# Query projection of a cross attention by row tile in place of by batch, and the last value projection moved ahead of the third sums

## The reference

```python
def _L0_xattn_ref(x, context, Wq, Wk, Wv):       # NHEADS = 32, HEAD_DIM = 16
    q = x @ Wq.T
    k_raw, v_raw = context @ Wk.T, context @ Wv.T
    q = q.reshape(b, n, NHEADS, HEAD_DIM).transpose(0, 2, 1, 3)
    kv = jnp.concatenate([k_raw, v_raw], axis=-1).reshape(b, m, NHEADS, HEAD_DIM, 2)
    k, v = (kv[..., i].transpose(0, 2, 1, 3) for i in range(2))
    q = _rmsnorm(q)                                # over the 16 of a head
    k = _rmsnorm(k)
    attn = jax.nn.softmax(jnp.einsum('bhnd,bhmd->bhnm', q, k) * scale, axis=-1)
    out = jnp.einsum('bhnm,bhmd->bhnd', attn, v)
```

## Time and profile before

| | us |
|---|---|
| Median of 3 runs | 1402.93 (1398.98 to 1403.82) |
| The profiled execution: its time | 1401.41 |
| its span, first to last instruction | 1399.3 |
| PE busy in the span | 1315.0 (94%), 10968 matmuls |
| DVE busy | 780.1 (56%) |
| ACT busy | 641.5 (46%) |
| POOL busy | 274.1 (20%) |
| Mean granted clock of PE | 0.984 |

### The profile page before, as it was taken

How to read it: one execution, slowest core, us unless ns; L and a number is a source line. 1 busy time by engine, 2 the same in 40 slices (tenths; PEclk the granted TensorE clock), 3 DMA queues, 4 the chain that set the end, 5 groups by cost and what they waited for, 6 DMA issues and landing times.

```text
span 1399.3 us, 27527 instructions
## 1 busy us (share of the span) xinstructions
PE 1315.0 (94%) x10968; PEld 868.8 (62%) x10968; DVE 780.1 (56%) x1938; ACT 641.5 (46%) x1452; POOL 274.1 (20%) x266
## 2 busy tenths in 40 slices
PE   4779999999999999999999999999999789999996
PEld 4656666666666666566666666666666445565543
DVE  3888775777677774534345444444345885444422
ACT  1443334333443335356666666666667222232321
POOL 0335441444444441211111112111111000000000
PEclk8989999999999999999999999999999999999999
DMA  8400000000000002011211111111213420000000
GB/s 258 143 25 1 1 1 1 1 1 2 1 1 1 1 1 112 22 68 49 70 61 46 45 45 45 45 45 46 66 47 122 155 87 23 0 23 1 22 1 28
DMA packets 22418, 59.99 MB, mean 43 GB/s; under 512 B 1177, under 2 KB 9369, under 8 KB 19091
## 3 DMA queue, kind: packets, MB, share of 16 engines
q1 hardware_dynamic: 22291, 58.24, 12.6%
HBM read 54.96 MB, written 3.28 MB: 42 GB/s over the span
## 4 chain that ended last, share of the span: by engine, by line
PE 83%; DVE 6%; issue 3%; ACT 1%; DVEq 0%; ACTq 0%
PE A L1592 21%; PE A L1505 11%; PE C L1914 10%; PE A L1559 10%; PE C L1616 6%; PE B L1633 5%; PE C L1545 3%; PE C L1530 3%; PE A L1930 2%; PE B L1930 2%; PE A L1514 2%; PE B L1601 2%; PE B L1538 2%; PE B L1522 2%; DVE qk L1113 1%
## 5 line engine op out<-in xcount | busy, mean ns | idle before, releaser
L1592 PE MATMUL A<-wxhl,arena 128*122 128x512 f16 x1152 | 265.3, 380 | 0.0
L1592 PEld LDWEIGHTS A<-wxhl,arena 128*122 128x122 f16 x1152 | 149.1, 134 | 88.0 <-issue 8.3
L1914 PE MATMUL C<-arena 128*128 128x375 f16 (+1 forms) x1024 | 185.9, 334 | 3.8 <-DVE arena L1114 3.8
L1505 PE MATMUL A<-arena,wxhl 128*125 128x512 f16 (+1 forms) x780 | 175.9, 383 | 6.8 <-DVE tub L953 5.0
L1914 PEld LDWEIGHTS C<-arena 128*128 128x128 bf16 x1024 | 99.6, 98 | 80.1 <-issue 6.4
L499 POOL TENSOR_TENSOR arena<-arena,region 100x512 f32<-100x512 f32 (+1 forms) x64 | 66.0, 1064 | 422.8 <-DVE region L1077 422.8
L1505 PEld LDWEIGHTS A<-arena,wxhl 128*125 128x125 f16 (+1 forms) x780 | 105.4, 137 | 66.9 <-DVE tub L953 5.4
L683 ACT ACTIVATE arena<-C 122x1600 f32<-122x1600 f32 x96 | 144.3, 1504 | 4.4 <-PE C L1616 2.8
L475 POOL TENSOR_TENSOR region<-tub 125x512 f32<-125x512 f32 (+1 forms) x65 | 82.6, 1271 | 277.4 <-DVE tub L953 277.3
L611 ACT ACTIVATE region<-C,negm 100x100 f32<-100x100 f32 x256 | 84.4, 356 | 102.2 <-DVE negm L997 102.2
L1559 PE MATMUL A<-arena,stageb 128*125 128x512 f16 (+1 forms) x416 | 123.8, 379 | 0.7 <-ACT arena L667 0.7
(11 more groups left out here) (163 smaller groups left out, 2092.4 us busy)
## 6 DMA issues: line engine op xcount, KB each, us to landing
stageb<-in_wffn SPq DMA_DIRECT2D x16, 768.0 KB, 4.7
arena<-in_ctxt SPq DMA_DIRECT2D x16, 722.0 KB, 4.7
stageb<-in_wffn SPq DMA_DIRECT2D x6, 1024.0 KB, 4.7
wxhl<-in_wffn SPq DMA_DIRECT2D x6, 1024.0 KB, 4.8
arena<-in_wqkv SPq DMA_DIRECT2D x4, 1024.0 KB, 22.4
arena<-in_wx SPq DMA_DIRECT2D x3, 1024.0 KB, 7.0
out_x<-xres SPq DMA_DIRECT2D x12, 250.0 KB
xres<-in_x SPq DMA_DIRECT2D x1, 2250.0 KB
```

Of the source, the lines that this page charges most:

```text
L1505: ins = pe.matmul(A[j % 2][0:m, :], xp[:, k, at:at + m], wp[:, j, k, :], start=(n == 0), stop=(n == 11))
L1592: ins = pe.matmul(A[(par + n) % 2][0:rows, :], lhs, wp[:, 0 if n == 0 else 1 if n < 4 else 2, k, :], start=(i == 0), stop=(i == 11))
L1914: ins = pe.matmul(C[2 * (e % 2) + half][:, 0:cols], wf[:, 3 * (e // 4) + half, k, (e % 4) * 128:(e % 4 + 1) * 128], part[:, k, 0:cols], st ...
```

## The change

The queries leave `project2` and `turn_heads` and get a path of their own by tile. `q_tile(b)` names the tile that batch b is the first to need: for all batches but 4, 9 and 14 there is one, 13 in all.

- `project_q(i)` projects the 125 rows of tile i with the same twelve matmuls, once per tile, at the end of a turn with an `x2_tile` (turns 0, 1, 3 to 6, 8 to 11, 13, and twice ahead of turn 0). Turns 2, 7 and 12 have none.
- `keep_q` (ACT) copies and squares the tile; the squares go to `sq`. `square_sums_q` (DVE) adds them up.
- POOL norms the queries first, with a signal of their own (`g_qn`), if the batch has a query tile, and the three key chunks.
- `turn_queries(i)` does the four query transposes of a tile into B0 right behind the sixth scores. `queries_back(i)` (DVE) copies all of them in one or two instructions, one for each batch in the tile, in place of four small ones per batch. The masked queries have two buffers now, `qms`, one for even batches (in `qk0`, free by then) and one for odd.
- `turn_heads` has key transposes only, and waits for the query copy once, since both use B0. `keys_back` waits for PE instead of DVE.
- The last value projection (`project2(b + 1, 6)`) and the first heads of batch b + 1 stand ahead of the third sums, on PE. On ACT the last value copy and the first key copy stand ahead of the third output copy.

The core of the diff:

```diff
+def q_tile(b):
+    return last_tile(b) if b == 0 or last_tile(b) > last_tile(b - 1) else None
...
-        qm = carve([128, NT, 2, S])
+        qm1 = carve([128, NT, 2, S])
...
+        qms = [qk0[:, :].rearrange("p g h s -> p (g h s)")[:, 0:NT * 2 * S]
+               .rearrange("p (t f s) -> p t f s", t=NT, f=2), qm1]
...
+            def keep_q(i, par):
+                rows = rows_of(i)
+                act.wait_ge(*count("pe_q", i, 1))
+                act.wait_ge(*count("pe_qT", i - 1, 1))
+                act.activation(raw[par][0:rows, 3], A[par][0:rows, :], ACT.Copy)
+                act.wait_ge(*count("d_ssqq", i - 1, 1))
+                act.activation(sq[0:rows, 0], A[par][0:rows, :], ACT.Square).then_inc(sig["a_sqq"], 1)
...
             def keys_back(b, t):
-                act.wait_ge(*count("d_T", b, t + 1))
+                act.wait_ge(*count("pe_T", b, t + 1))
...
                 exp2(b, 5)
+                if end < 2:
+                    values(b + 1, 2, odd)
+                    keys_back(b + 1, 0)
                 out_back(b, 2)
-                if end < 2:
-                    keys_back(b + 1, 0)
-                    values(b + 1, 2, odd)
...
-                if end < 1:
-                    keep_raw(b + 2, 0, par)
+                if x2_tile(b) is not None:
+                    keep_q(x2_tile(b), par)
...
-            def queries_back(b, t):
-                dve.wait_ge(*count("pe_T", b, t + 1))
-                dve.wait_ge(*count("pe_sc", b - 1, T_UNITS[t]))
-                q = B[0][:, CTXP:CTXP + S].unsqueeze(1).broadcast_to([128, 2, S])
-                parity = cst[:, C_PAR:C_PAR + 2].unsqueeze(2).broadcast_to([128, 2, S])
-                dve.tensor_tensor(qm[:, t], q, parity, ALU.mult).then_inc(sig["d_T"], 1)
+            def queries_back(i):
+                n = rows_of(i)
+                dve.wait_ge(*count("pe_qT", i, 1))
+                for b, lo, hi, at in pieces(i):
+                    if b > 1:
+                        dve.wait_ge(*count("pe_sc", b - 2, NU))
+                    q = B[0][:, 0:NT * n].rearrange("p (t s) -> p t s", t=NT)[:, :, at:at + hi - lo]\
+                        .unsqueeze(2).broadcast_to([128, NT, 2, hi - lo])
+                    parity = cst[:, C_PAR:C_PAR + 2].unsqueeze(1).unsqueeze(3).broadcast_to([128, NT, 2, hi - lo])
+                    ins = dve.tensor_tensor(qms[b % 2][:, :, :, lo:hi], q, parity, ALU.mult)
...
-                if end < 2:
-                    queries_back(b + 1, 0)
+                if end < 2 and q_tile(b + 1) is not None:
+                    queries_back(q_tile(b + 1))
...
+            def project_q(i, par):
+                m, at, n = rows_of(i), i % 4 * TW, 0
+                pe.wait_ge(*count("d_x2", i, 1))
+                for xp, wp in ((x2h, wxh), (x2h, wxl), (x2l, wxh)):
+                    for k in range(KT):
+                        ins = pe.matmul(A[par][0:m, :], xp[:, k, at:at + m], wp[:, 0, k, :], start=(n == 0), stop=(n == 11))
+                        n += 1
+                ins.then_inc(sig["pe_q"], 1)
...
+            def turn_queries(i, par):
+                n = rows_of(i)
+                pe.wait_ge(*count("g_qn", i, 1))
+                for t in range(NT):
+                    ins = pe.transpose(B[0][:, t * n:(t + 1) * n], raw[par][0:n, 3, t * 128:(t + 1) * 128], ident[0:n, 0:n])
+                ins.then_inc(sig["pe_qT"], 1)
...
             pe.wait_ge(*count("a_v2", 0, 3))
-            project_out(TL - 1, b, A[0])
-            pe.wait_ge(*count("a_pT", b, 4))
+            def between(g):
+                if g == 2:
+                    pe.wait_ge(*count("a_pT", b, 4))
+                    turn_queries(0, 0)
+            project_out(TL - 1, b, A[0], between)
+            pe.wait_ge(*count("d_qT", 0, 1))
             turn_heads(0, 0, 0)
             pe.wait_ge(*count("a_T", 0, 1))
-            pe.wait_ge(*count("d_T", 0, 1))
...
                 scores2(b, 5)
-                attend2(b, 2, par)
                 if end < 2:
                     if o2_tile(b) is not None:
                         pe.wait_ge(*count("d_on", o2_tile(b), 1))
+                    if q_tile(b + 1) is not None:
+                        turn_queries(q_tile(b + 1), odd)
+                    project2(b + 1, 6, odd)
+                    if q_tile(b + 1) is not None:
+                        pe.wait_ge(*count("d_qT", q_tile(b + 1), 1))
                     turn_heads(b + 1, 0, odd)
-                    project2(b + 1, 6, odd)
+                attend2(b, 2, par)
+                if end < 2:
                     scores2(b + 1, 0)
                 attend2(b, 3, par)
...
-                if end < 1:
-                    project2(b + 2, 0, par)
+                if x2_tile(b) is not None:
+                    pe.wait_ge(*count("a_v2", b + 1, 2))
+                    project_q(x2_tile(b), par)
```

140 lines of the change are left out of this document (67 added, 73 removed).

## The result

The changed kernel takes **1395.87 us** (median of 14 runs, 1392.47 to 1398.53), the kernel before on the same chips 1401.84 (14 runs, 1398.87 to 1404.02). The ratio is **0.9952, with a 95% interval from 0.9941 to 0.9963**: 5.2 to 8.3 us less by the interval, in which the quotient of the two medians, 0.9957, lies too. The forecast was 1400.5, or 2.4 us less, with a range from 1394.5 to 1407. So the time lies in the range, but near its lower end, and the gain is more than twice the forecast's. The profiled execution takes 1395.92 us with a span of 1394.1, against 1401.41 and 1399.3 before: 5.2 us of span to find.

The account below looks back on a forecast made before the run. PE was taken to bound the kernel. Eight turns +1.3, turns 3, 8, 13 -1.1, turns 2, 7, 12 -2.2, turn 14 +1.0, entry -0.5, exit -0.9 gave -2.4 us: 1400.5 from the median 1402.9, range 1394.5 to 1407.

Parts of the forecast that it names:

- The wait: Turns 2, 7, 12: PE waits 1.7 us for ACT's second key copy before the output transposes; -2.2 us in all.
- The division before S: DVE's output division ends 0.07 us before S, the end of the sixth scores, so PE's query transposes do not wait.
- The query copy: DVE can start it 0.6 us after the sixth scores end; wanted at 3.22, it takes 1.36 to 1.85: no wait.
- The key copy: ACT's first key copy ends 4.30 us after the sixth scores end; the scores want it at 4.75, margin 0.45: no wait.
- Turn 14's wait of 1.1 us: PE waits before the keys for DVE's query copy, held up by row scales; turn 14 costs +1.0 us in all.
- The hand-overs: PE from keys to sums and sums to scores: taken as 0; could cost 2.1 us or give back 0.6.
- the clock's hold: Entry: shorter waits may spare 1.9 us, giving 1393.5 if ACT's wait is missing too; missing wait with or without clock: 0.18.
- The exit: Turn 15: DVE starts the weight scales 1.5 us sooner, but ACT's copy ending at 1084.38 leaves 0.9: -0.9 us.
- The missing wait: Rival: ACT keeps up in turns 2, 7, 12, so another 5.1 us stay: 1395.4; chance 0.18 with or without the clock.
- the three new waits: Rival, turns 2, 7, 12: the clock falls at each of PE's waits for ACT, 1.9 us each: 1406.2; chance 0.15.
- The slow copy: Rival: DVE's query copy decides above 2.6 us; at 3.4 us, 9.6 us more over 12 turns: 1410.1; chance 0.12.
- The change does less: Rival: entry and exit give nothing, +1.4 us: 1401.9; chance 0.55 together with the forecast and its hand-overs.

Follow-up runs that it names:

- experiment 3: The changed kernel with twelve unused matmuls of a query projection's size put back into turns 2, 7 and 12: 1398.14 us, ratio 0.9971 to the kernel before.
- experiment 7: The changed kernel with every DVE query copy made twice: 1403.51 us, ratio 1.0003 to the kernel before.
- experiment 8: The changed kernel with ACT's copy of the first keys behind the third output copy: 1408.70 us, ratio 1.0050 to the kernel before.
- experiment 4: The changed kernel with DVE's query copy ahead of the row scales in turn 14: 1396.33 us, ratio 0.9960 to the kernel before.
- Experiment 1: The kernel before with only the new order on PE and ACT, queries still by batch: 1401.81 us, ratio 0.9993 to the kernel before.
- experiment 6: The changed kernel with DVE waiting for turn 15's last heads before the weight scales: 1397.66 us, ratio 0.9965 to the kernel before.
- experiment 12: The changed kernel with turn 14's query copy ahead of row scales, and ACT's context copy behind the second key copy in turns 2, 7, 12: 1398.88 us, ratio 0.9972.
- experiment 5: The changed kernel with the first tile's query transposes behind the output projection instead of within it: 1399.83 us, ratio 0.9979 to the kernel before.
- experiment 9: The changed kernel with ACT's context copy ahead of the third output copy (turns 2, 7, 12), key copy ahead of the fourth (also turn 14): 1396.69 us, ratio 0.9960.

## Why the prediction was right or wrong

**The sign and the mechanism were right.** PE sets the time of cross attention, 3 x 2.59 us of projection go, and ACT's queue takes most of it back (3 x 1.63). The wait stands where forecast, in turns 2, 7 and 12, released by the copy of the second keys. Its length is 1.36 us and not 1.7. By experiment 3 its price is 1.63: I had worked out when ACT's queue ends, and the end was right to 0.24 us (8.84 forecast for the copy's hand-over, 8.60 measured: 1007.63 against S at 999.03). What I called the wait was counted from start to start (1.5 by that measure), and the profile counts idle time only from the end of the last matmul.

**Terms that were mis-sized in the turns (1.3 us together).** The query transposes cost 0.48 to 0.49 us, not 0.53, and the projection behind them 2.60, not 2.69, while the keys ahead of the sums cost 0.41, not 0.36: 10.19 against 10.28 in each of eight turns, 0.7 of the 1.3. ACT's two output copies took 0.27 to 0.29 from start to start, not 0.40 as their busy time has it; twice 0.12, and as the other terms of the queue cancel, that is how much earlier its end came. The output transposes behind the wait take 0.10 of it back (0.63 and not 0.53), and with the rounding of my sum 0.16 are left in each of turns 2, 7 and 12. I priced PE from start to start, and in ACT's queue took busy times for two of the terms.

**Margins.** All three held. The division before S: no wait before the query transposes in any turn. The query copy: wanted 2.39 us after its start, takes 1.26, and experiment 7 shows where it would have become a wait. The key copy: margin 0.41. Forecast and experiment 8 agree that it is the thinnest one. Turn 14's wait of 1.1 us is 1.03 in the trace, and experiment 4 confirms its cause and shows its price, 1.25; so the change could have had 1.2 us more in cross attention by one move on DVE.

**The hand-overs.** Keys to sums take 0.41 us from start to start and sums to scores 1.16 (1002.11, 1002.52, 1003.68): 0.05 more than the keys cost before, and 0.01 less than the sums did. The projection gives way to keys 0.09 sooner than it did to scores, which pays for it. Experiment 1, which has the new order and nothing else, gives 9.93 against 9.94. The Trainium skill (TensorEngine Tiling (Array Packing), Key Properties) says that a change of the tiling mode drains TensorE. With as many changes as before it leads one to expect no difference, and 9.93 against 9.94 agrees. No run here has more such changes than the kernel before, so their price stays unseen.

**The entry: a term put at nothing.** The waits fell as forecast, -0.5. But I gave the clock's hold a small chance and tied it to the absence of the other wait, as one rival. The two do not hang together: ACT's wait formed, and the clock held all the same. It held at the entry in all ten profiles with the shorter entry, and fell in the four with a longer one: before, the move alone, the entry as before, and the copy made twice, whose entry has only one wait of 0.20 us more. So -1.7 us belonged in the sum with a chance of its own. There is one profile of each kernel but the changed one, which has two, and at other places falls come and go between executions of one kernel; so 14 of 14 make the link with the waits likely, and how much waiting the clock bears there is not shown. The Trainium skill (TensorE: Matmul & The Clock Gate, Part 4) has transposes not counting as busy for the clock. I used it as an argument against the clock's hold, and there it misled me: transposes and waits still fill the entry from 593.22 to 595.93, and the clock stays at 1.00. Whether transposes count can't be told from these runs; what they show is that the clock fell in the one profile with 0.20 us more of waiting, and in those with more than that.

**The exit: forecast -0.9, measured -1.6.** That DVE would start 1.5 us sooner was right (1.57). The step that failed is "0.9 stays". I held ACT's copy at 1083.79 fixed while everything ahead of it moved. That copy hangs on PE's transposes of the third tile, which come 8.20 us behind turn 14's output transposes and not 9.62. Of these 1.42 us, 1.03 are a hole that I had not seen. PE in turn 15 of the kernel before:

```profile
1080.64 1.23 PE L1633 MATMUL B<-arena 122*32 122x100 f32 x47
1082.90 0.27 PE L1633 MATMUL B<-arena 122*32 122x100 f32 x1 [1.03 <-issue]
```

The last of 48 matmuls stands back for 1.03 us, and nothing in the profile releases it. The move alone has it too (0.89 us, at 1082.59), and it is in none of the profiles with tile-wise queries. What makes it is open. DVE is the bound there by experiment 6, so the hole could have counted only through ACT's copy.

**The rivals.** The missing wait: it formed. The clock did not fall at the three new waits in any kernel that has them as the change left them, and that each stands alone is the likely reason: in experiment 12 it does fall at two of three such places, where waits of 0.65 and 1.44 us have only 1.6 us of work between them. The slow copy had 1.26 us against the 2.6 from which it was to decide. "The change does less" was wrong on both counts, entry and exit. The time lies in the range, but not for the reason that the range gave: its lower end was set low for the case in which ACT's wait is missing, and it was the clock, the exit and the mis-sized terms of the turns that brought the time there. These come to 3.8 us, and an early stage that happened to be 1.0 us longer hid a part of them. So that the time lies in the range is in part luck.

**What stays open.** 6.0 us by the medians and 5.2 by the spans agree only within a fall or two of the clock: after fell once less than before in the first profile, and as often in the second (four against four). The early stage also lies 1.0 us apart between profiles of the same code. So the places above are sure to 0.1 us each, and the total to about 2 us. Where the clock fell is known for the profiled executions alone. Over all executions on record the mean granted clock is 0.984 for the changed kernel (19) and 0.983 for the kernel before (72), 0.982 with the entry as before (experiment 5, 10 executions), but 0.983 in experiment 4 (6), whose entry is short: these means do not prove a fall at the entry, nor speak against it. The gain is not the clock's alone, though: at the highest clock that both show, 0.987, the kernel before has spans of 1396.0 to 1397.5 us and the changed one of 1390.7 and 1390.8.

## What to carry to other kernels

When a change removes work from the bounding engine, write down the queue of the engine that then ends last from start to start, with the same measure for every term; and count a wait at its idle time plus 0.1 to 0.3 us, so that one of 0.2 costs twice what it shows. Give a stretch with several short waits, where the clock falls, a chance of its own in the sum: here the entry with 0.8 us less of waiting was worth another 1.7 us. Before work is moved into a gap of such a queue, look at what the pushed-back instruction releases: the wait can come back through the other engine (experiment 9). And work that is deferred must be followed to its reader (experiment 12).

## What the runs showed that I had not expected

- **A wait costs more than its idle time.** 1.36 shown, 1.63 paid (experiment 3); 1.03 and 1.25 (4); 0.19 and 0.41 (7); 0.82 and 0.90 (8).
- **The clock's falls move between profiles of one kernel.** The changed kernel fell at 225, 382 and 1090, and in its second profile at 225, 382, 538 and 1155. Where the same code ran without the falls at 225 and 382 (experiments 6 and 8), the first keys started at 589.61 and 589.99 and not at 593.22: 1.6 to 1.8 us a fall. That is larger than most of the effects under study, and a reason to read parts of turns and not totals.
- **Behind a fall PE pays by the half-speed stretch, not by the wait:** projections of 2.6 us took 4.45, 4.54, 3.95, 3.78 and 4.28.
- **A copy out of PSUM through four dimensions is not slow:** 800 elements a partition take 0.99 us, 600 take 0.78, 400 take 0.57, 200 take 0.37: about 1.03 ns an element and 0.16 us besides.
